# Spreading query rows to edges with 16-bit one-hots and query rows in three 16-bit parts

## The reference: what is computed

```python
# layer 0 (e0): a number per node and head from either end, and one from the edge
alpha = a_src[src_a] + a_dst[dst_a] + a_edge
alpha = jnp.where(alpha > 0, alpha, NEG_SLOPE * alpha)
# layer 2, first half (e21): a product of two rows per head
alpha = jnp.einsum('ehc,ehc->eh', q[dst], k[src]) / np.sqrt(ch)
# both: softmax over the edges of a target, and the sum of the values with it
m = jax.ops.segment_max(alpha, dst, num_segments=n)
ea = jnp.exp(alpha - m[dst])
denom = jax.ops.segment_sum(ea, dst, num_segments=n)
out = jax.ops.segment_sum((ea / denom[dst])[:, :, None] * v[src], dst, num_segments=n)
```

## Time and profile before

| | us |
|---|---|
| median of three runs | 4744.84 |
| profiled execution, its own time | 4744.87 |
| span from its first to its last instruction | 4741.9 |
| TensorE busy in the span | 2848.9 (60%) |
| VectorE busy | 2989.2 (63%) |
| GpSimd busy | 2723.8 (57%) |
| ScalarE busy | 936.1 (20%) |

### The profile page before, as it was taken

The page is one execution under the profiler, slowest core; times in us unless marked ns, Lnnn a source line. Parts: engine busy times, 40 slices in busy tenths (PEclk is TensorE's granted clock), DMA queues, the critical chain, the costliest instruction groups (busy, mean ns, idle before and its releaser), DMA issues. The chain is left out here.

```text
span 4741.9 us, 55842 instructions
## 1 busy us (share of the span) xinstructions
PE 2848.9 (60%) x18074; PEld 2638.2 (56%) x18075; DVE 2989.2 (63%) x6166; ACT 936.1 (20%) x769; POOL 2723.8 (57%) x2656
## 2 busy tenths in 40 slices
PE   1366665666505566555568246666666657995865
PEld 0355665565504555545458145665666657884744
DVE  6365565556576666666660457777777777996243
ACT  0121122122111222222220021122212213441000
POOL 0577777777607777777770077777777733552000
PEclk9565666666556676777779667777777778996978
DMA  0444444444414454444550255655565534450432
GB/s 20 113 97 105 109 101 98 109 106 97 99 29 111 131 134 134 134 134 131 137 140 20 49 136 149 153 148 147 149 153 148 147 80 104 114 119 2 168 109 74
DMA packets 169180, 526.15 MB, mean 111 GB/s; under 512 B 60576, under 2 KB 87525, under 8 KB 156195
## 3 DMA queue, kind: packets, MB, share of 16 engines
q1 hardware_dynamic: 73757, 299.78, 25.4%
q0 software_dynamic: 95264, 224.28, 18.3%
HBM read 456.40 MB, written 67.48 MB: 110 GB/s over the span
## 5 line engine op out<-in xcount | busy, mean ns | idle before, releaser
L547 POOL DMA_INDIRECT e21G<-table,e21src x858 | 852.7, 994 | 504.5 <-issue 258.9
L547 POOL DMA_INDIRECT e0G<-table,e0src x858 | 852.4, 994 | 435.9 <-issue 401.2
L1344 POOL DMA_INDIRECT t1G<-table,t1idx x806 | 789.1, 979 | 375.8 <-issue 242.9
L1417 PE MATMUL t1psW<-t1CO,t1G 128*128 128x192 f32 x1612 | 426.8, 427 | 314.5 <-issue 301.0
L1417 PEld LDWEIGHTS t1psW<-t1CO,t1G 128*128 128x128 f32 x1612 | 362.7, 254 | 322.0 <-issue 307.1
L571 PE MATMUL e21psQ<-Q,e21OT 121*128 x1716 | 412.4, 409 | 141.0 <-DVE e21G L685 53.1
L571 PEld LDWEIGHTS e21psQ<-Q,e21OT 121*128 121x128 f32 x1716 | 399.8, 326 | 152.8 <-issue 94.2
L564 PE MATMUL e0psQ<-Q,e0OT 121*128 x1716 | 398.7, 371 | 94.2 <-ACT e0OT L602 58.0
L564 PEld LDWEIGHTS e0psQ<-Q,e0OT 121*128 121x128 f32 x1716 | 396.6, 325 | 99.7 <-issue 99.7
L1939 POOL TENSOR_TENSOR e22Z<-e22Z,e22C 121x847 f32<-121x847 f32 (+1 forms) x104 | 200.1, 1956 | 261.0 <-ACT e22Z L1931 261.0
L587 PE MATMUL e21psA<-e21G,e21O 128*121 128x145 f32 x1716 | 275.4, 332 | 106.1 <-DVE e21G L736 106.1
(11 more groups left out here) (428 smaller groups left out, 5336.0 us busy)
## 6 DMA issues: line engine op xcount, KB each, us to landing
e0dstb<-in_dst_p SPq DMA_DIRECT2D x27, 1996.5 KB
e21dstb<-in_dst_p SPq DMA_DIRECT2D x27, 1996.5 KB
e22C<-counts SPq DMA_DIRECT2D x26, 1487.0 KB
Q<-in_type_p SPq DMA_DIRECT2D x62, 416.0 KB
counts<-X SPq DMA_DIRECT2D x13, 1487.0 KB
planes<-SKIP SPq DMA_DIRECT2D x26, 743.5 KB
counts<-RES SPq DMA_DIRECT2D x13, 1487.0 KB
e31C<-planes SPq DMA_DIRECT2D x26, 743.5 KB
```

The lines of the kernel that those rows point to most:

```text
L547: nc.gpsimd.indirect_dma_start(out=G[:, u, t, 0:width], out_offset=None, in_=table, in_offset=bass.IndirectOffsetOnAxis(ap=src[:, u, t:t + ...
L1344: nc.gpsimd.indirect_dma_start(out=G[:, q % 2, t, :], out_offset=None, in_=table, in_offset=bass.IndirectOffsetOnAxis(ap=idx[:, q * GT + t ...
L1417: mmi = nc.tensor.matmul(psW[:, k % 2, 0:WIN * NBAS], G[:, q % 2, t, :], CO[:, k % 2, i].rearrange("p w b -> p (w b)"), start=(i == 0), st ...
```

## The change

`OT` becomes 16-bit (its 0 and 1 are exact). The query rows of a block are taken apart into three 16-bit parts (`QP`) whose sum is the fp32 row: the first is the row rounded, the second the rest rounded, the third what is left of that. A tile's spread is then three matmuls with the same weights that add up in fp32, where it was one fp32 matmul in two halves. The parts are made on VectorE by `query_parts`, for the next step, between the values and `prepare`; for step 0 ahead of the loop. TensorE no longer reads the block number; VectorE reads it once more. TensorE waits for the new semaphore `parts_ready` behind `targets_ready`.

```diff
@@ -469,7 +469,9 @@
         dst3 = sb("dst3", [128, T + 2], I32)
         dstb = sb("dstb", [BN, CH], I32)
         dstf = sb("dstf", [128, T + 2])
-        OT = sb("OT", [BN, CH])
+        OT = sb("OT", [BN, CH], BF16)
+        QP = sb("QP", [BN, 2, 3, QW], BF16)
+        qr = sb("qr", [BN, QW])
         O = sb("O", [128, T, BN])
         ne = sb("ne", [128, T + 1])
         rb = sb("rb", [128, T + 1])
@@ -502,7 +504,7 @@
         psB = ctx.enter_context(nc.psum_tensor(name + "psB", [128, 512], F32))
         names = ("waited", "rows_wanted", "scores_made", "edges_in", "edges_used", "slots_free", "spread_ready", "spread_free", "targets_ready", "ends_ready",
                  "ends_turned", "carry_ready", "carry_turned", "diff_ready", "weights_done", "values_ready",
-                 "sums_done", "sums_free", "merge_ready", "merge_done", "pe_waited", "consts", "squared", "one_set")
+                 "sums_done", "sums_free", "merge_ready", "merge_done", "pe_waited", "consts", "squared", "one_set", "parts_ready")
         S = {n: sem(n) for n in names}
         gathered = [[sem(f"gathered{u}{b}") for b in range(NG)] for u in range(2)]
         sources_in = [sem(f"sources_in{u}") for u in range(2)]
@@ -554,22 +556,24 @@
             with pe.Fori(0, g["n_pairs"](pe)) as i:
                 for u in range(2):
                     s = i * 2 + u
-                    blk = pe.value_load(g["steps_i"][0:1, bass.ds(s, 1)], min_val=0, max_val=NB - 1)
                     pe.wait_ge(S["targets_ready"], s + 1)
+                    pe.wait_ge(S["parts_ready"], s + 1)
                     onehot = OT[:].rearrange("d (p t) -> d t p", t=T)
                     if gat:
                         pe.wait_ge(S["spread_free"], s + 1)
                         for t in range(T):
 
-                            mmi = nc.tensor.matmul(psQ[:, u, t * QW:(t + 1) * QW], onehot[:, t, :],
-                                                   Q[:, bass.ds(blk, 1), 0:QW].rearrange("p a f -> p (a f)"), start=True, stop=True)
+                            for k in range(3):
+                                mmi = nc.tensor.matmul(psQ[:, u, t * QW:(t + 1) * QW], onehot[:, t, :], QP[:, u, k, :],
+                                                       start=(k == 0), stop=(k == 2))
                         mmi.then_inc(S["spread_ready"], 1)
                     for b, tiles in enumerate(BATCH if not gat else ()):
                         pe.wait_ge(S["spread_free"], s * NG + b + 1)
                         for j, t in enumerate(tiles):
 
-                            mmi = nc.tensor.matmul(psQ[:, b % 3, j * QW:(j + 1) * QW], onehot[:, t, :],
-                                                   Q[:, bass.ds(blk, 1), 0:QW].rearrange("p a f -> p (a f)"), start=True, stop=True)
+                            for k in range(3):
+                                mmi = nc.tensor.matmul(psQ[:, b % 3, j * QW:(j + 1) * QW], onehot[:, t, :], QP[:, u, k, :],
+                                                       start=(k == 0), stop=(k == 2))
                         mmi.then_inc(S["spread_ready"], 1)
                     pe.wait_ge(S["ends_ready"], s + 1)
                     for k in range(6):
@@ -667,6 +671,21 @@
                 V.tensor_tensor(O[:, t0:t1, :], bc(g["iota"][:, 0:BN].unsqueeze(1), [128, t1 - t0, BN]),
                                 bc(dstf[:, 1 + t0:1 + t1].unsqueeze(2), [128, t1 - t0, BN]), ALU.is_equal)
 
+            def query_parts(s, u):
+
+                blk = dve.value_load(g["steps_i"][0:1, bass.ds(s, 1)], min_val=0, max_val=NB - 1)
+                q = Q[:, bass.ds(blk, 1), 0:QW].rearrange("p a f -> p (a f)")
+                V.tensor_copy(QP[:, u, 0, :], q)
+                dve.drain()
+                V.tensor_tensor(qr[:], q, QP[:, u, 0, :], ALU.subtract)
+                dve.drain()
+                V.tensor_copy(QP[:, u, 1, :], qr[:])
+                dve.drain()
+                V.tensor_tensor(qr[:], qr[:], QP[:, u, 1, :], ALU.subtract)
+                dve.drain()
+                V.tensor_copy(QP[:, u, 2, :], qr[:]).then_inc(S["parts_ready"], 1)
+
+            query_parts(0, 0)
             prepare(0, 0)
             match(0, T)
             with dve.Fori(0, g["n_pairs"](dve)) as i:
@@ -735,6 +754,7 @@
                         v = G[:, u, t0:t1, vo:vo + D].rearrange("p t (h c) -> p t h c", h=H)
                         V.tensor_tensor(v, v, bc(G[:, u, t0:t1, wo:wo + H].unsqueeze(3), [128, t1 - t0, H, C]), ALU.mult).then_inc(S["values_ready"], 1)
 
+                    query_parts(s + 1, 1 - u)
                     prepare(s + 1, 1 - u)
                     for b, tiles in enumerate(BATCH):
                         dve.wait_ge(S["slots_free"], s * NG + (2 * NG + b + 1))
```

## The result

The changed kernel takes 4878.7 us in the median of 4 runs (4874.69 to 4880.02), the kernel before, on the same chip, 4746.1 us (4738.65 to 4753.8): ratio 1.0278, 95% interval 1.026 to 1.0296. That is 133 us slower, where 51 had been forecast; the sign was right, the time lies 53 us above the range. The profiled execution has a span of 4876.0 us against 4741.9, 134.1 more.

The account below looks back on a forecast made before the run. It took circles of gathers, VectorE work and loads to bound both passes, not TensorE's spread. 4744.87 us plus 16 for the first pass (e0) and 35 for the second (e21) gave 4796, range 4762 to 4826.

Parts of the forecast that it names:

- Spread at nothing: TensorE's new spread, 99 matmuls near 100 ns, 10 us a step, stays within its cover and costs nothing.
- The rival of the strided read at 232 ns: Strided 16-bit weights keep the fp32 pace on TensorE, 23.0 us a step, late in the second pass: 4825 us; chance 0.09.
- The rival that the 4.17 us wait in e21 is for the spread: VectorE's second-pass wait is for the spread, not gathered rows, so a shorter spread saves time: 4697 us; chance 0.07.
- Price of the five instructions: Added on VectorE between values and `prepare`: 1.2 us a step in the first pass, 1.65 in the second.
- The sequencer's load of the block number: VectorE's read is covered by running values, costing nothing; rival: uncovered, 0.5 us a step, 4815 us, chance 0.07.
- the one-hots in 2 bytes: Same number of elements on ScalarE, so 3.82 us as before.
- e0, a half of the addition: First pass: the circle closes over two steps, so each step gets half of 1.2 us, 0.6; 16 us in all.
- the circle: First-pass loop: gathers, scores, VectorE's memset signal, SP's loads, source list, gathers again; 87.07 us for two steps.
- e21, 1.35 us a step: Second pass: addition of 1.65 us less 0.1 hidden behind ScalarE and 0.2 returned; 35 us in all.
- the circle is one step long: Second pass: VectorE's 23.01 us and 20 us of loads make the 43.00 us period, so additions count every step.
- a return of only 0.2: Second pass: later loads let VectorE do the fifth group before its wait; between 0 and 1.40 us, taken as 0.2.
- The change part by part: Prediction's section pricing the spread, five VectorE instructions, block number read, added wait and one-hots, then summing them.

Follow-up runs that it names:

- parts_once: Changed kernel with the parts of all blocks made once ahead of each pass and TensorE reading the block number again: 4744.02 us, ratio 0.9998 to before.
- shift_after: Changed kernel plus eight drains, run once ahead of the second pass's loop, only to move its code: 4789.32 us, ratio 1.0092 to before.
- parts_twice: Kernel before with the query rows split twice in every step, the parts unused, no drains added: 4890.69 us, ratio 1.0313 to before.
- parts_unused: Kernel before with the parts computed each step but unused, spread still fp32, eight drains ahead of the second pass's loop: 4789.30 us, ratio 1.0093.

## Why the prediction was right or wrong

*Spread at nothing: right.* parts_once has it alone, at ratio 0.9998. The estimate of 100 ns a matmul was too high (61 ns in e0; in e21 36 of them in 2.43 us, 68 ns each), with no effect on the sum. The rival of the strided read at 232 ns is refuted by the row of 99 matmuls in 6.01 us, and the rule of the Trainium skill that the prediction weighed against it ("TensorE: Matmul & The Clock Gate", weight-path perf modes) agrees with the trace for strided 16-bit weights too. The rival that the 4.17 us wait in e21 is for the spread is refuted too: with the 16-bit spread VectorE waits 4.3 us for it and 110.8 for rows (shift_after), and in parts_once the wait for the fifth group's rows is 4.96 us a step against 4.71 before (means over 24 steps).

*Price of the five instructions: right.* 1.22 and 1.54 us against 1.2 and 1.65. The sequencer's load of the block number stayed covered: no idle time stands ahead of L678 in the loops. Uncovered, as the second one of parts_twice is, it costs 0.45 to 0.52 us a step, the rival's 0.5. The added wait showed nothing, and the one-hots in 2 bytes take ScalarE the same 3.82 us.

*e0, a half of the addition: nearly.* 0.85 us a step where 0.6 was forecast. Over 22 steps of before and of parts_unused the circle's parts are: signal to first gather 21.0 and 21.15, gathers 42.5 and 42.5, last gather to scores 1.77 and 2.08, scores to signal 22.12 and 23.36. The sums are 87.4 and 89.1, half the difference is 0.86. So the half was right, but the circle lengthened by 1.7 and not by 1.2: of the 0.5 us more, the scores' later start behind the last gather is 0.3. That the later loads meet the end of the gathers would explain it and is not shown.

*e21, 1.35 us a step: too much.* It was 0.92. The step that failed is "the circle is one step long", with a return of only 0.2: 0.6 of the 1.54 us came back. It did not come from the fifth group's wait alone. That fell by about 1.05 us a step, from 4.71 to 3.66, but the sixth group's rose from 0.01 to 0.94 (means over 24 steps of before and of shift_after), as the prediction had said of the next group. All of VectorE's waiting at the group multiply fell by 0.33 us a step, from 5.69 to 5.36, and the rest came from shorter waits elsewhere, 0.2 of it ahead of `match`. GpSimd, which had waited 4 times for the list of sources, now did 18 times. This fits gathers that were the longer circle by about half a microsecond, so that the first part of VectorE's addition was free; no run shows that by itself. Both passes and the rest together: 45 us of span (4787.1 - 4741.9, shift_after) against 51 forecast. With these sizes the forecast would have stood at 4790, inside its range.

*The term that was missing, and the step that put the time outside the range: the place of the code.* "The change part by part" prices what the added instructions do, on every engine and queue, and puts the room that they take at nothing, without a reason. They lengthened a loop and moved it, and 89 of the 134 us are VectorE waiting for its own code (4876.0 - 4787.1). The trace of before could not give a size for it: its loops in these passes show no instruction packets. But that a loop has a place was to be seen, and the range had no bound for it.

## What to carry to other kernels

When an edit lengthens a loop on an engine, look in the new trace for idle time labelled "issue" behind the loop's last instruction and for packets in the instruction queue; if they are there, time the same kernel with a few drains ahead of the loop before you judge the edit. Where an engine has slack, work is cheapest behind the signal that starts the next transfers: the same five instructions cost 44 us ahead of it and 13 behind it. And if a small transfer is queued behind a large one and closes a circle, move it to the front: 26 us here.

## What the runs showed of the hardware

Eight drains, run once, are worth 89 us, and 48 cost 98. A jump that has to wait for code took 8.4 to 11.4 us while a 2 MB load and gathers ran, with a second wait behind it in e21 (6.7 us in the turn shown), and 1.9 us where no data moved. In e0 a jump of 10.7 us cost only some 0.56 us a step, since VectorE waited there anyway and the profile put the wait down to the gather.

TensorE's fp32 spread kept 232 ns a matmul at 0.57 and at 1.00 of the clock, the 16-bit one 61 ns at 0.76, with the same stride of 33 elements: a quarter of the time for each matmul with half the bytes a weight, and three matmuls in place of two for each tile.
